# Attention and quantised feed-forward on one core: the order of TensorE's units regrouped by array shape

## The chip, the cores and the metric

The kernel runs on one core of a Trainium2 chip. The metric is the device time of one launch in microseconds, the median over runs. A profiled execution of the kernel before gives every row of the trace that is shown here.

## What is computed

Four sequences of 1024 rows of 128 numbers are normalised, go through attention with 16 heads of 64 columns, and through a quantised linear layer; the sum of input and both results is the output.

```
xn = layernorm(x)
q, k, v = heads(xn @ Wq), heads(xn @ Wk), heads(xn @ Wv)
w = softmax(q k^T / 64 + causal);  w = w * clip((key_no + span * 1024) / 33, 0, 1)
w = w / (sum(w) + 1e-8)
out = x + heads_back(w v) @ Wo + quantised(xn) @ (ternary - 1)^T + bias
```

## The kernel before, in words

**Rounds.** Two heads form a pair; there are 32 pairs, eight for each sequence (a "batch" in the code). The kernel runs about one round for each pair. Each engine has a written order of work (PE_PLAN, ACT_PLAN, DVE_PLAN, POOL_PLAN, SP_PLAN, lines 36 to 41, with _FIRST and _LAST for the ends), a list of words. `walk` goes through the list once for each pair i; a "+" behind a word means pair i + 1, a "-" pair i - 1. `happens` says in which pairs the rare words occur. Nothing but semaphores ties the engines together, and each engine works strictly in its order.

**TensorE's units.**

- Q, K (`projection`): the pair's queries and keys, 12 products of 512 columns together; V (`values`): 12 products of 256 columns; X0, X1 (`turn`): the transposed rows of the next sequence, three times in the run. All use the full array of 128 x 128.
- M0 to M11 (`max_unit`, L968): raw scores from which row maxima are taken, one product for each of the two heads. S0 to S11 (`scores_of`, L1006): the real scores by key block in transposed form, four products for each head, 512, 384, 256 or 128 columns wide (on the diagonal of the causal mask). Both use the array as two halves of 64 rows, one for each head.
- G3, G7, G11 (`value_products`, L1023): weights times values for tiles 0 to 3, 4 to 7 and 8 to 11 into the bank `pv`. D0, D1 (`denominators`, L1038): the sums of the weights for both halves of the queries. Both use the array as two halves of 64 columns.
- Y0, Y1 (`output_projection`, L1065; L1053 is the quantised product, which the last pair of a sequence puts ahead of it) and T (`turn_maxima`): the full array.

**Banks.** M, S, Q, K and V units go through `ring`, three slots of two banks. `slot_left` makes each unit wait until the unit three places earlier in the ring has been read: an S by ACT's exponential E, an M by DVE's maxima R, a Q or K by its low parts, a V by DVE's Vs.

```python
n = PLACE[name, i]
unit, j = IN_RING[n - NSLOT]
if unit[0] == "S":
    pe.wait_ge(exp_done, tiles_upto(j, int(unit[1:])))
elif unit[0] == "M":
    pe.wait_ge(max_read, j * NM + int(unit[1:]) + 1)
```

T, D, Y, X and W go through the one bank `beside` (`beside_left`): a Y waits until the D ahead has been turned into reciprocals, and a second Y until the first has been added to the output.

**The other engines.** ACT: E0 to E11 (exponentials, L567), copies of Q and K (L556), the logarithm and its exponential (ln, ex) of the denominators. DVE: R0 to R11 (L768 twice for a diagonal unit, L772 once for R4 to R7), low parts of Q and K (L744), Vs (L755), t, u, o (L792, L797, L804), the additions Ya0 and Ya1 to the output (L813), one step q of the quantisation in seven rounds of eight. GpSimd (POOL): L (causal selection, L474) and A (running sums of the weights, L495 to L501), the bias B. D0 waits for A3, D1 for A11; G3 to G11 wait for the selections L. SP issues the DMAs that place rows of maxima and keys.

Of the kernel before, what the change touches and what calls it, by code (L numbers as in the profile page):

```python
# [22 lines left out]
N_PAIRS = 32  # L23
# [82 lines left out]
IN_RING = [("X", -2)] + [u for u in PE_ORDER if u[0][0] in "QKSMV" or u == ("D1", LAST)]  # L106
IN_BESIDE = [u for u in PE_ORDER if u[0][0] in "THDYXWF" and u not in (("D1", LAST), ("Y1", LAST))]
# [23 lines left out]
def attention_ffn(nc, x_dram, wq_dram, wk_dram, wv_dram, wo_dram, span_dram, tern_dram, bias_dram,  # L131
# [11 lines left out]
    with ctx:  # L143
# [243 lines left out]
        def _(pool):  # L387
# [78 lines left out]
            pool.wait_ge(maxrow_done, 1)  # L466
            add_bias(0)
# [36 lines left out]
            for name, i in walk(POOL_PLAN, "", POOL_LAST):  # L504
                if name[0] == "L":
                    select(i, int(name[1:]))
                elif name[0] == "A":
                    add(i, int(name[1:]))
                else:
                    add_bias((6, 11, 14).index(i) + 1)  # L510

        @block.scalar
        def _(act):
# [29 lines left out]
            def turned_whole(b, c, src):  # L543

                if b > 0:
                    act.wait_ge(fq_step, (b - 1) * FQ_STEPS + 1)
                else:
                    act.wait_ge(x2_done, c + 1)
# [47 lines left out]
            for name, i in walk(ACT_PLAN, ACT_FIRST):  # L596
# [32 lines left out]
        def _(dve):  # L629
# [212 lines left out]
            for name, i in walk(DVE_PLAN, DVE_FIRST, DVE_LAST):  # L842
# [35 lines left out]
        def _(pe):  # L878
            t_ = nc.tensor

            def slot_left(name, i):
# [11 lines left out]
                elif unit == "V":  # L893
                    pe.wait_ge(v_done, j + 1)
                else:
                    pe.wait_ge(xf_done, 2)

            def beside_left(name, i):
# [13 lines left out]
                elif unit[0] == "X":  # L912
                    pe.wait_ge(x2_done, 2 * batch_of_turn(j) + int(unit[1:]) + 1)
# [164 lines left out]
            for name, i in PE_ORDER:  # L1078
# [27 lines left out]
                elif name[0] == "X":  # L1106
                    turn(batch_of_turn(i), int(name[1:]), beside[:, :])
# [28 lines left out]
```

## Time and profile before

| | |
|---|---|
| median of 3 runs | 1001.96 us (1001.88 to 1002.1) |
| the profiled execution | 1001.64 us, its span 999.9 us |
| granted clock, mean | 0.997 |
| PE busy | 985.0 us, 99%, 7121 instructions |
| DVE busy | 757.3 us, 76% |
| POOL busy | 707.5 us, 71% |
| ACT busy | 451.7 us, 45% |
| chain that ended last | PE 87%, DVE 8%, issue 2%, POOL 1%, ACT 1%, DMA 1% |

The profiled execution spends 1.74 us outside its span and lies 0.32 us under the median. In the timeline, a row's first number is the start from the span's beginning and the second its length. TensorE's products overlap in the pipeline and their ends are modelled, so the distance from one start to the next is what counts there. A row's "xN" merges N instructions of one line.

### The profile page before, as it was taken

To read this page: it belongs to the slowest core of one execution; us is meant where nothing else is said; L and a number is where in the kernel's file an instruction comes from. 1 tells how busy PE (TensorE), PEld (TensorE's weight loads), DVE (VectorE), ACT (ScalarE), POOL (GpSimd) and SP (SyncE) were. 2 spreads that over 40 slices of the span, in tenths; PEclk is the share of its full clock that TensorE was granted. 3 is DMA by queue.
4 is the path that set the end of the run, shared out by engine and by line. 5 is a ranking of instruction groups with operands and counts; after the bars stand their busy time and mean duration, and the time that the engine had idled before them with its cause. 6 is when DMAs were issued, how large, how long until landed. Compare 5 with 4: busy or idle time off the path is not lost.

```text
span 999.9 us, 19209 instructions
## 1 busy us (share of the span) xinstructions
PE 985.0 (99%) x7121; PEld 634.2 (63%) x7121; DVE 757.3 (76%) x1706; ACT 451.7 (45%) x607; POOL 707.5 (71%) x649
## 2 busy tenths in 40 slices
PE   8899999999999999999999999999999999999997
PEld 4666666666666666666666666666666666666654
DVE  7877888878788878777767777777877667777754
ACT  4344445444454444454443454444454444454442
POOL 8766867667767668767767767667767667777672
PEclk9999999999999999999999999999999999999999
DMA  6000000000000000000000000000000000000000
GB/s 176 3 2 2 2 1 3 2 3 2 2 22 3 2 2 2 1 3 2 3 12 13 1 3 2 2 2 3 1 2 23 3 2 2 1 2 2 2 2 22
DMA packets 16133, 8.52 MB, mean 9 GB/s; under 512 B 5404, under 2 KB 15644, under 8 KB 16040
## 3 DMA queue, kind: packets, MB, share of 16 engines
q1 hardware_dynamic: 15416, 7.15, 2.7%
q8 instruction: 57, 0.93, 0.4%
q14 instruction: 36, 0.29, 0.1%
q10 hardware_dynamic: 624, 0.14, 0.1%
HBM read 4.33 MB, written 2.10 MB: 6 GB/s over the span
## 4 chain that ended last, share of the span: by engine, by line
PE 87%; DVE 8%; issue 2%; POOL 1%; ACT 1%; DMA 1%; DVEq 0%; SPq 0%; ACTq 0%; POOLq 0%
PE pv L1023 25%; PE ring L1006 24%; PE ring L968 12%; PE beside L1065 7%; PE beside L1038 6%; PE ring L941 3%; PE ring L937 3%; PE ring L938 3%; DVE ring L768 3%; DVE v L755 2%; DVE beside L792 1%; PE ring L955 1%; PE beside L1053 1%; PE ring L956 1%; PE ring L957 1%
## 5 line engine op out<-in xcount | busy, mean ns | idle before, releaser
L567 ACT ACTIVATE prob<-ring 128x1024 f32<-128x1024 f32 (+3 forms) x384 | 293.6, 810 | 347.9 <-PE ring L1006 347.7
L501 POOL TENSOR_TENSOR psumd<-psumd,prob 128x512 f32<-128x512 f32 (+1 forms) x250 | 406.4, 1626 | 28.9 <-POOL psumd L501 1.3
L768 DVE CUSTOM_DVE_ANT_0 ring<-ring,causal 128x128 f32<-128x128 f32 (+3 forms) x512 | 240.3, 517 | 96.7 <-PE ring L968 96.2
L1006 PE MATMUL ring<-q,k 64*128 64x512 f32 (+3 forms) x2304 | 279.5, 347 | 1.7 <-DMA mrow<-maxrow 0.8
L1023 PE MATMUL pv<-prob,v 128*64 128x512 f32 (+3 forms) x1536 | 267.1, 490 | 0.0
L474 POOL TENSOR_SCALAR_AFFINE_SELECT prob<-prob 128x256 f32<-128x256 f32 x256 | 110.1, 432 | 216.1 <-ACT prob L567 214.1
L1006 PEld LDWEIGHTS ring<-q,k 64*128 64x128 f32 x2304 | 194.6, 185 | 37.3 <-DVE rowmax L768 5.1
L1023 PEld LDWEIGHTS pv<-prob,v 128*64 128x64 f32 x1536 | 104.9, 137 | 154.1 <-issue 142.4
L772 DVE TENSOR_REDUCE rowmax<-ring 128x2 f32<-128x1024 f32 x128 | 151.5, 1222 | 4.8 <-PE ring L968 1.3
L497 POOL TENSOR_TENSOR psumd<-prob 128x768 f32<-128x768 f32 (+1 forms) x63 | 132.6, 2105 | 24.3 <-ACT prob L567 19.1
L968 PE MATMUL ring<-k,q 64*128 64x512 f32 (+3 forms) x768 | 143.9, 410 | 4.2 <-DVE k L744 1.5
L1006 PE MATMUL ring<-mrow,kext 64*128 64x512 f32 (+3 forms) x768 | 133.6, 342 | 0.0
L968 PEld LDWEIGHTS ring<-k,q 64*128 64x128 f32 x768 | 64.9, 184 | 74.2 <-ACT prob L567 27.7
L556 ACT ACTIVATE q<-ring 128x1024 fp32r<-128x1024 f32 x32 | 32.9, 1028 | 143.6 <-PE ring L941 143.6
L1006 PEld LDWEIGHTS ring<-mrow,kext 64*128 64x128 f32 x768 | 73.2, 185 | 7.7
L1065 PE MATMUL beside<-wo,o 128*128 128x128 f32 x512 | 73.4, 286 | 1.1 <-DVE o L804 1.1
L768 DVE DVE_READ_ACCUMULATOR2_ANT rowmax<- 128x1 f32 x512 | 72.5, 142 | 0.0
L1065 PEld LDWEIGHTS beside<-wo,o 128*128 128x128 f32 x512 | 62.0, 191 | 13.9 <-issue 9.2
L792 DVE TENSOR_TENSOR beside<-beside,r 128x512 f32<-128x512 f32 x63 | 45.0, 715 | 32.9 <-ACT r L578 32.8
L744 DVE TENSOR_TENSOR q<-ring,q 128x1024 fp32r<-128x1024 f32 x32 | 39.1, 1222 | 40.1 <-ACT q L556 40.0
L1038 PE MATMUL beside<-psumd,ones 128*64 128x512 f32 x252 | 68.0, 617 | 0.9 <-POOL psumd L501 0.9
L937 PE MATMUL ring<-x,w 128*128 128x512 f32 x128 | 53.0, 414 | 0.0
(120 smaller groups left out, 947.0 us busy)
## 6 DMA issues: line engine op xcount, KB each, us to landing
kext<-kext SPq DMA_DIRECT2D x128, 4.0 KB, 1.7
out<-x_sb SPq DMA_DIRECT2D x8, 256.0 KB, 2.4
x_sb<-in_L_attn_query SPq DMA_DIRECT2D x3, 512.0 KB, 5.5
mrow<-maxrow SPq DMA_DIRECT2D x62, 4.0 KB
x_sb<-in_L_attn_query SPq DMA_DIRECT2D x2, 256.0 KB, 4.0
xn_sb<-in_L_attn_Wv SPq DMA_DIRECT2D x1, 512.0 KB, 5.5
wo<-in_L_attn_Wo SPq DMA_DIRECT2D x1, 512.0 KB, 7.0
xn_sb<-in_L_attn_Wq SPq DMA_DIRECT2D x1, 448.0 KB, 3.5
```

The source lines that it names most:

```text
L474: g.affine_select(out=d, in_=d, compare_op=ALU.is_ge, fill=0.0, base=0, pattern=[[0, 2], [1, P]], channel_multiplier=-1).then_inc(sel_done, 1)
L497: g.tensor_tensor(acc[:, :, lo:HALF], before[:, :, lo:HALF], pr[:, :, lo:HALF], ALU.add).then_inc(acc_done, 2)
L501: g.tensor_tensor(acc[:, :, lo:HALF], acc[:, :, lo:HALF], pr[:, :, lo:HALF], ALU.add).then_inc(acc_done, 1)
L567: a.activation(prob[n % NPROB][:, :, lo:HALF], ring[:, slot(f"S{t}", i), :, lo:HALF], ACT.Exp, scale=1.0 / DH).then_inc(exp_done, 1)
L768: last = v.tensor_tensor_reduce(out=ring[:, s, h, 0:n], in0=ring[:, s, h, 0:n], in1=causal[:, HALF - n:HALF], scale=1.0, scalar=MASKED, op ...
L772: last = v.tensor_reduce(dst[:, :, 0], ring[:, s, :, 0:n], axis=AX, op=ALU.max)
L937: t_.matmul(ring[:, s, c, :], w1[n][:, cols], xa[:, rows], start=True, stop=False)
L968: last = t_.matmul(ring[:, s, h, 0:n], q1[p][rows, j * P:(j + 1) * P], k1[p][rows, k0:k0 + n], start=True, stop=True)
L1006: last = t_.matmul(ring[:, s, h, lo:HALF], k[p][rows, keys], q[p][rows, cols], start=(at == 0), stop=(at == len(parts) - 1))
L1023: last = t_.matmul(pv[h * DH:(h + 1) * DH, lo:HALF], v_sb[i // 2 % 2][:, kb, i % 2 * 2 + h, :], prob[(i * NT + t) % NPROB][:, h, lo:HALF], ...
L1038: last = t_.matmul(out[h * DH:(h + 1) * DH, :], ones[:, :], psumd[c][:, h, :], start=True, stop=not direct)
L1065: last = t_.matmul(beside[:, k * P:(k + 1) * P], o_sb[c][:, k * P:(k + 1) * P], wo[:, i % NPB, :], start=not with_ffn, stop=(not with_ffn ...
```

## The change

The written orders are changed, and with them three details: the transposed rows X of the next sequence (both halves as one unit) go through the ring instead of `beside`; their unsplit copy xf is made by GpSimd as the sum of the two parts and not by two copies of ACT; and the first bias is added in round 0 instead of ahead of the rounds.

TensorE's steady round, with "|" at each change of the array's shape, before and after:

```
T Q K | G11 | M0 M1 S0 S1 S2 M2 | D1 | M3 S3 | V | S4 S5 M4 S6 M5 | Y1 | M6 M7 S7 | D0 G3 |
  M8 S8 S9 S10 M9 | Y0 | M10 M11 S11 | G7 |
T Q K | G11 D1 | M0 M1 S0 S1 S2 S3 S4 M2 M3 | Y0 V (X) Y1 | M4 S5 S6 M5 S7 M6 M7 | D0 G3 |
  M8 S8 S9 S10 M9 M10 M11 S11 | G7 |
```

```diff
-PE_PLAN = ("T Q+ K+ X0 X1 W G11- M0+ M1+ S0 S1 S2 M2+ D1- M3+ S3 V+ S4 S5 M4+ S6 M5+ Y1- M6+ M7+ S7 D0 G3 "
-           "M8+ S8 S9 S10 M9+ Y0 M10+ M11+ S11 G7")
-ACT_PLAN = "Z Qhi+ Khi+ X0 X1 E0 E1 E2 ln1- ex1- E3 E4 E5 E6 E7 ln0 ex0 E8 E9 E10 E11"
-DVE_PLAN = ("Tc Z Qlo+ Klo+ R0+ R1+ X0 X1 W R2+ R3+ t1- u1- Vs+ o1- R4+ R5+ Ya1- R6+ R7+ t0 u0 R8+ o0 q "
-            "R9+ R10+ Ya0 R11+")
-POOL_PLAN = "L0 A0 L1 A1 L2 A2 L3 A3 A4 A5 A6 A7 L8 L9 L10 L11 A8 A9 A10 A11 B"
+PE_PLAN = ("T Q+ K+ G11- D1- M0+ M1+ S0 S1 S2 S3 S4 M2+ M3+ Y0- V+ X Y1- M4+ S5 S6 M5+ W S7 M6+ M7+ D0 G3 "
+           "M8+ S8 S9 S10 M9+ M10+ M11+ S11 G7")
+ACT_PLAN = "Z Qhi+ Khi+ ln1- ex1- E0 E1 E2 E3 E4 X E5 E6 E7 ln0 ex0 E8 E9 E10 E11"
+DVE_PLAN = ("Tc Z Qlo+ Klo+ q R0+ R1+ t1- u1- o1- R2+ Ya0- R3+ Vs+ X R4+ Ya1- W R5+ R6+ R7+ t0 u0 R8+ o0 "
+            "R9+ R10+ R11+")
+POOL_PLAN = "L0 L1 L2 A0 L3 A1 A2 A3 B0 A4 A5 A6 A7 L8 A8 L9 L10 L11 A9 A10 A11 B xf"
 
 PE_FIRST = ("Q+ K+ I0+ I1+ M0+ M1+ M2+ I2+ M3+ I3+ M4+ I4+ M5+ I5+ H+ M6+ I6+ M7+ I7+ M8+ I8+ M9+ I9+ M10+ I10+ "
-            "M11+ S0+ S1+ T+ S2+ S3+ Q++ K++ V+")
+            "M11+ S0+ S1+ T+ S2+ S3+ Q++ K++ V+ S4+ M0++ I11+ M1++ I12+")
...
-ACT_FIRST = "xf0+ Qhi+ xf1+ Khi+ keys+ rest+ Hrow+ wv+ E0+ E1+ E2+ E3+ Qhi++ Khi++"
+ACT_FIRST = "xf0+ Qhi+ xf1+ Khi+ keys+ rest+ Hrow+ wv+ E0+ E1+ E2+ E3+ Qhi++ Khi++ E4+"
...
-PE_LAST = "T G11- S0 S1 S2 D1- S3 S4 S5 S6 Y1- S7 D0 G3 S8 S9 S10 S11 Y0 D1 F1 G7 G11 Y1"
+PE_LAST = "T G11- D1- S0 S1 S2 S3 S4 Y0- S5 Y1- S6 S7 D0 G3 S8 S9 S10 S11 Y0 D1 F1 G7 G11 Y1"
...
-DVE_LAST = "Tc t1- u1- o1- A5 Ya1- A6 A7 t0 u0 o0 A8 A9 Ya0 t1 u1 o1 Ya1"
+DVE_LAST = "Tc t1- u1- o1- q Ya0- A5 Ya1- A6 A7 t0 u0 o0 A8 A9 Ya0 t1 u1 o1 Ya1"
...
+BIAS_AT = (0, 6, 11, 14)
...
-    if name in ("X0", "X1"):
-        return i % PAIRS_OF_BATCH == 4 + int(name[1:]) and i < N_PAIRS - PAIRS_OF_BATCH
+    if name in ("X", "xf"):
+        return i % PAIRS_OF_BATCH == (4 if name == "X" else 5) and i < N_PAIRS - PAIRS_OF_BATCH
...
-IN_RING = [("X", -2)] + [u for u in PE_ORDER if u[0][0] in "QKSMV" or u == ("D1", LAST)]
-IN_BESIDE = [u for u in PE_ORDER if u[0][0] in "THDYXWF" and u not in (("D1", LAST), ("Y1", LAST))]
+IN_RING = [("X", -2)] + [u for u in PE_ORDER if u[0][0] in "QKSMVX" or u == ("D1", LAST)]
+IN_BESIDE = [u for u in PE_ORDER if u[0][0] in "THDYWF" and u not in (("D1", LAST), ("Y1", LAST))]
...
-            pool.wait_ge(maxrow_done, 1)
-            add_bias(0)
+            def rows_of_parts(b):
+
+                pool.wait_ge(x2_done, 2 * b + 2)
+                pool.wait_ge(fq_step, (b - 1) * FQ_STEPS + 1)
+                g.tensor_tensor(xf[:, :], x1[b % 2][:, :].bitcast(F32), x2[b % 2][:, :].bitcast(F32), ALU.add
+                                ).then_inc(xf_done, 2)
...
-                elif name[0] == "X":
-                    turned_high(batch_of_turn(i), int(name[1:]), beside[:, :])
-                    turned_whole(batch_of_turn(i), int(name[1:]), beside[:, :])
+                elif name == "X":
+                    for c in range(2):
+                        turned_high(batch_of_turn(i), c, ring[:, slot("X", i), c, :])
...
-                    quantise(i // NPB, i % NPB + 1)
-                elif name[0] == "X":
-                    turned(batch_of_turn(i), int(name[1:]), beside[:, :])
+                    quantise(i // NPB, i % NPB)
+                elif name == "X":
+                    for c in range(2):
+                        turned(batch_of_turn(i), c, ring[:, slot("X", i), c, :])
...
-                elif name[0] == "X":
-                    turn(batch_of_turn(i), int(name[1:]), beside[:, :])
+                elif name == "X":
+                    for c in range(2):
+                        turn(batch_of_turn(i), c, ring[:, slot("X", i), c, :])
```

## Rows read from the trace of the kernel before

**Rows 1.** Windows view: length, then busy time (instructions) per engine, PEclk, DMA.

```profile
903.98:933.72 29.74, 29.73 (x221) 19.25 (x219) 21.95 (x49) 13.59 (x18) 21.20 (x20) 1.00 0.01 2
...
36.00:39.00 3.00, 1.41 (x11) 0.86 (x9) 3.00 (x6) 0.13 (x1) 2.92 (x3) 0.96 0.01 1
39.00:42.00 3.00, 3.00 (x13) 2.30 (x14) 3.00 (x14) 0.00 (x0) 1.53 (x3) 0.50 0.01 3
```

**Rows 2.** Timeline of TensorE: start, length, line, operation, count.

```profile
914.11 0.39 PE L955 MATMUL ring<-wv,x 128*128 128x256 f32 x1
...
914.45 0.28 PE L957 MATMUL ring<-wv,x 128*128 128x256 f32 x1
...
915.51 0.28 PE L957 MATMUL ring<-wv,x 128*128 128x256 f32 x1
915.72 0.99 PE L1006 MATMUL ring<-q,k 64*128 64x512 f32 x6
...
916.76 0.89 PE L1006 MATMUL ring<-q,k 64*128 64x512 f32 x6
...
917.89 0.50 PE L968 MATMUL ring<-k,q 64*128 64x512 f32 x2
918.22 0.85 PE L1006 MATMUL ring<-q,k 64*128 64x512 f32 x6
...
919.13 0.40 PE L968 MATMUL ring<-k,q 64*128 64x512 f32 x2
919.46 1.16 PE L1065 MATMUL beside<-wo,o 128*128 128x128 f32 x8
920.55 0.74 PE L968 MATMUL ring<-k,q 64*128 64x512 f32 x4
```

**Rows 3.** Timeline of TensorE, M0 after G11, then M3 and S3 after D1.

```profile
909.37 0.50 PE L968 MATMUL ring<-k,q 64*128 64x128 f32 x4
...
913.28 0.50 PE L968 MATMUL ring<-k,q 64*128 64x512 f32 x2
913.62 0.45 PE L1006 MATMUL ring<-q,k 64*128 64x128 f32 x6
```

**Rows 4.** Timeline of TensorE, from S10 to Y0.

```profile
927.14 0.52 PE L1006 MATMUL ring<-q,k 64*128 64x256 f32 x6
...
927.73 0.38 PE L968 MATMUL ring<-k,q 64*128 64x256 f32 x2
928.04 1.16 PE L1065 MATMUL beside<-wo,o 128*128 128x128 f32 x8
```

**Rows 5.** Timeline of ScalarE: E6, then E8 to E10, then E9 alone.

```profile
919.34 1.02 ACT L567 ACTIVATE prob<-ring 128x1024 f32<-128x1024 f32 x1 [0.40 <-PE ring L1006]
...
926.65 2.22 ACT L567 ACTIVATE prob<-ring 128x1024 f32<-128x1024 f32 x3 [2.12 <-PE ring L1006]
...
927.58 0.80 ACT L567 ACTIVATE prob<-ring 128x768 f32<-128x768 f32 x1
```

**Rows 6.** Timeline of VectorE: R3, Vs, R4 with R5, Ya1, end of R9.

```profile
913.98 0.70 DVE L768 CUSTOM_DVE_ANT_0 ring<-ring,causal 128x512 f32<-128x512 f32 x1 [0.30 <-PE ring L968]
...
915.24 0.73 DVE L792 TENSOR_TENSOR beside<-beside,r 128x512 f32<-128x512 f32 x1
...
916.62 1.22 DVE L755 TENSOR_TENSOR v<-ring,vtab 128x1024 f32<-128x1024 f32 x1
...
918.54 2.37 DVE L772 TENSOR_REDUCE rowmax<-ring 128x2 f32<-128x1024 f32 x2
920.83 0.68 DVE L813 TENSOR_TENSOR x_sb<-x_sb,beside 128x512 f32<-128x512 f32 x1
...
929.04 0.14 DVE L768 DVE_READ_ACCUMULATOR2_ANT rowmax<- 128x1 f32 x1
```

**Rows 7.** Timeline of GpSimd: L0, and the last addition, A11.

```profile
911.93 0.41 POOL L474 TENSOR_SCALAR_AFFINE_SELECT prob<-prob 128x256 f32<-128x256 f32 x1 [3.92 <-ACT prob L567]
...
937.29 0.74 POOL L501 TENSOR_TENSOR psumd<-psumd,prob 128x256 f32<-128x256 f32 x1 [0.43 <-POOL psumd L501]
```

More of the change, by code:

```diff
@@ L79, in happens @@
     if name == "q":
-        return i % PAIRS_OF_BATCH < PAIRS_OF_BATCH - 1
+        return i % PAIRS_OF_BATCH > 0
     if name == "Z":
@@ L83, in happens @@
     if name == "B":
-        return i in (6, 11, 14)
+        return i in BIAS_AT[1:]
+    if name == "B0":
+        return i == BIAS_AT[0]
     if name == "store":
@@ L508, in _ @@
                     add(i, int(name[1:]))
+                elif name == "xf":
+                    rows_of_parts(batch_of_turn(i - 1))
                 else:
-                    add_bias((6, 11, 14).index(i) + 1)
+                    add_bias(BIAS_AT.index(i))
         @block.scalar
@@ L541, in turned_high, with turned_whole @@
                 a.activation(x1[b % 2][:, c * HALF:(c + 1) * HALF], src, ACT.Copy).then_inc(x1_done, 1)
[L543 to L548, printed above, removed]
+            def turned_whole(c, src):
+                act.wait_ge(x2_done, c + 1)
                 a.activation(xf[:, c * HALF:(c + 1) * HALF], src, ACT.Copy).then_inc(xf_done, 1)
@@ L604, in _ @@
                     inverses(i, int(name[2:]))
-                elif name[0] == "X":
-                    turned_high(batch_of_turn(i), int(name[1:]), beside[:, :])
-                    turned_whole(batch_of_turn(i), int(name[1:]), beside[:, :])
+                elif name == "X":
+                    for c in range(2):
+                        turned_high(batch_of_turn(i), c, ring[:, slot("X", i), c, :])
                 elif name[:2] == "xf":
-                    turned_whole(0, int(name[2:]), ring[:, slot("X", -2), int(name[2:]), :])
+                    turned_whole(int(name[2:]), ring[:, slot("X", -2), int(name[2:]), :])
                 elif name == "rest":
@@ L672, in turned @@
                 cols = slice(c * HALF, (c + 1) * HALF)
-                dve.wait_ge(x1_done if b == 0 else xf_done, 2 * b + c + 1)
+                dve.wait_ge(x1_done, 2 * b + c + 1)
                 v.tensor_tensor(x2[b % 2][:, cols], src, x1[b % 2][:, cols].bitcast(F32), ALU.subtract
@@ L894, in slot_left @@
                     pe.wait_ge(v_done, j + 1)
+                elif j < 0:
+                    pe.wait_ge(xf_done, 2)
                 else:
-                    pe.wait_ge(xf_done, 2)
+                    pe.wait_ge(x2_done, 2 * batch_of_turn(j) + 2)
             def beside_left(name, i):
@@ L911, in beside_left @@
                     pe.wait_ge(y_added, halves_upto(j, int(unit[1:])))
-                elif unit[0] == "X":
-                    pe.wait_ge(x2_done, 2 * batch_of_turn(j) + int(unit[1:]) + 1)
                 else:
```

## The prediction, made before the changed kernel ran

> **What bounds the kernel now.** The windows view comes first. In a steady round of 29.74 us TensorE is busy for 29.73, DVE for 21.95, GpSimd for 21.20, ACT for 13.59 [rows 1], so a round is what TensorE's order takes. A busy TensorE is not one at its peak, however: what it loses stands between the starts of its instructions, and for that I read its timeline unit by unit. There are two kinds of loss.
>
> *A change of the array's shape.* V's pieces follow each other every 0.118 us: nine steps from 914.45 to 915.51. Twelve would take 1.41, but V takes 1.61 until S4 starts: some 0.10 is lost as it starts and 0.09 as it leaves. S4, first after the change, takes 1.04 (915.72 to 916.76), while S6, as wide and inside its shape, takes 0.91 or 0.92 (918.22 to 919.13): 0.12 lost in the restart. M5, a pair as wide as those of S6 (0.23 each), takes 0.33 before Y1: 0.10 on the way in [rows 2]. So one excursion from the row shape into the full array and back costs 0.10 + 0.20 + 0.12 = 0.42 us. D1's excursion: 0.10 in and 0.09 out (taken as for M5 and V), and M3 after it 0.34 for a pair of 0.23 [rows 3], 0.11: together 0.30.
>
> *A slot that is still being read.* M9 may only start when E8 has read S8's slot. E8 ends at 926.65 + 1.03 = 927.68 [rows 5], M9's first instruction is at 927.73, and Y0 follows 0.31 later [rows 4], for a pair of 256 columns that takes 0.12, with 0.09 for the change behind it. The other 0.10 is M9's own start: its weights were not loaded ahead. So **a unit that was held streams 0.15 us after its release**, and I call that its effective start. M4, behind V's slot and so behind Vs, shows the same from the other side: S5 takes 1.13 for 0.92, and M4 0.33 for 0.23 [rows 2], a wait of 0.31 in all.
>
> **The change, part by part, in a steady round.**
>
> *1. Fewer changes of shape.* The full-array units inside the scores (V, Y1, Y0) were three excursions and become one: 2 x 0.42 = 0.84 saved. D1 joins G11: 0.30 saved. Sum -1.14 us. The products themselves are the same, moved. The Trainium skill, "TensorEngine Tiling (Array Packing)", Key Properties, says that changing the tiling mode drains TensorE; these rows agree with it, and by that rule alone a round would take 28.60.
>
> *2. The excursions were also pauses for the readers of the ring.* The same page, PSUM Bottleneck, says that tiling speeds up TensorE but not the evacuation of PSUM. What the rows make of that is worked out here from the readers' own times; by the page's rule alone no number follows. I lay the measured durations into the new order, with three slots.
>
> (a) After G3: M8 S8 S9 S10 M9 M10 M11 S11. M9's effective start is 927.83, as before. M10 takes S9's slot, so it waits for E9, which ends at 927.58 + 0.80 = 928.38 [rows 5]: effective 928.53 in place of 927.83 + 0.12 = 927.95, **wait 0.58**. M11 waits for E10: three exponentials end at 926.65 + 2.22 = 928.87 [rows 5], effective 929.02 in place of 928.53 + 0.17 = 928.70, **0.32**. S11 waits for R9, ended at 929.04 + 0.14 = 929.18 [rows 6]: 929.33 in place of 929.02 + 0.23, **0.08**. Today Y0 stands behind M9 and covers all of these.
>
> (b) S0 S1 S2 S3 S4 in a row. An exponential starts 1.12 after its S (E6 919.34, S6 918.22 [rows 2, 5]), the first lasts 1.03, the second ends 0.70 later (928.38 less 927.68). Counted from S0, S3 starts effectively at 1.12 + 1.03 + 0.15 = 2.30, held by E0, where M2 stands today with the same wait: no difference. S4 is held by E1: 2.15 + 0.70 + 0.15 = 3.00. S3 takes 0.49 less the 0.09 of the change behind it (913.62 to 914.11 [rows 2, 3]), so S4 would have started at 2.70: **0.30**.
>
> (c) S5 S6 M5 S7. S7 now takes S5's slot: E5 ends 1.12 + 1.02 after S5, effective 2.29, against 0.92 + 0.92 + 0.23 = 2.07: **0.22**.
>
> (d) M6 M7. M7 now takes M5's slot, and R5 stands at the end of an unbroken run of DVE. Ya0 starts about 1.1 after Y0's effective start (seven pieces, and some 0.3 for the result, an estimate). On DVE the next instruction starts 0.09 before the last has ended (R4 and R5 take 2.37 together for 1.23 each), so from start to start Ya takes 0.68 - 0.09 = 0.59, R3 1.26 (913.98 to 915.24), Vs 1.22 - 0.09 = 1.13, R4 1.14 [rows 6]. R5 could then start at 1.1 + 0.59 + 1.26 + 1.13 + 1.14 + 0.59 = 5.81. TensorE: Y0 0.90 (1.09 less its two losses), V 1.41, Y1 0.90, change 0.19, M4 0.23, S5 0.92, S6 0.92: M5 at 5.47; R5 starts 0.55 after it (R4 918.54, M4's effective start 917.99 [rows 2, 6]), at 6.02, ends at 7.25, M7 effective at 7.40. Without R5, M7 would follow S7 (3.63 + 2.29 = 5.92), 0.92 and M6's 0.23: 7.07. **Wait 0.33.**
>
> Sum of new waits: 0.58 + 0.32 + 0.08 + 0.30 + 0.22 + 0.33 = +1.83 us. M4's old wait goes, because its slot is now M2's, read long before: -0.31.
>
> *3. What stays hidden.* D1 right behind G11 needs A11 earlier. A11 ends at 938.03 [rows 7]; its round's T, where the windows are cut, stood at 933.72 and D1 would start where M0 stands now, 5.39 behind T (909.37 less 903.98 [rows 1, 3]), at 939.11. Slack 1.1 us, minus 0.15; and A8 is pulled ahead of L9 to L11. The bias additions and xf, at most 3.0 us each (four times A11's 0.74 for 256 columns of two operands), come in six rounds and go into GpSimd's idle time before L0, 3.92 us [rows 7]; B0 alone stands in mid-round, once. If that cover were gone, D1 would be late by the difference. q on DVE now stands ahead of R0, in the time of G11 and D1. ACT loses six copies. ln and ex now stand ahead of E0 and fit between D1's end and E0, which must wait for S0 in any case: 0. SP's DMAs of the row maxima get a microsecond more. All this at 0, between -0.1 and +0.2 a round.
>
> *4. The ends.* Y0 of round 0 moves out of the first round and that of round 30 into the last: 0. The fill-in products I11 and I12 and the earlier S4, M0, M1 may keep the clock up in the start: today TensorE is busy for 1.41 of 3 us and then runs at a granted clock of 0.50, the lower level of 1.2 GHz, for the next 3.00 us [rows 1], which costs up to 1.5. I take -1. The three rounds with X have ACT's and DVE's reading of X inside the run of (d); I take +0.3 each, +1. Together 0, bounds -3 and +3.
>
> **The sum.** +1.83 - 0.31 - 1.14 = +0.38 us in each of 31 rounds: +11.8. 1001.64 (the profiled execution, 0.32 under the median) + 11.8 = 1013.4, **1013.5 us**. Each wait rests on three or four starts read to 0.05; 0.25 on their sum is 8 us. Its own range is 1004 to 1022.
>
> **The rivals.**
>
> *The drain alone counts.* None of the new waits shows, since a reader catches up inside the run: -1.45 x 31 = -45, **957 us**. For it: ACT is busy 13.59 of 29.74 us, DVE 21.95 [rows 1]. Against it: M9 and M4 show a held unit waiting to the hundredth although both engines have idle time. It decides wherever the new waits come to less than 1.45 a round, against the 1.83 found. If only group (a) failed to show, 0.98 less, the time would be 1013.5 - 30 = **983 us**. Chance 0.14 for all of this side.
>
> *An even trade.* Waits of 1.45: 1002 us. 0.06.
>
> *GpSimd becomes the bound.* D1 is held by A11. It needs GpSimd 1 us later than now against T; L1 and L2 ahead of A0 wait for later exponentials, and the bunch at S5 starts late. Were it 1 us beyond the slack, 31 us more on the forecast: **1044 us**. 0.05.
>
> *The forecast*, slower by the waits of the bunches: 0.75.
>
> The three runs lie within 0.22 us; a difference of 0.2%, 2 us, is about what a measurement of this kernel can tell from no change. Faster 0.15, same 0.06, slower 0.79. Range 998 to 1022: it leaves out the rivals at 957, 983 and 1044 and holds the even trade.
>
> **What would show it.** Right: a steady round of 30.1 us; M10 held by E9 and M11 by E10 in the waits, some 0.9 us a round together; M7 by R5; S4 by E1; M4's wait for Vs gone; D1 not waiting for POOL. Wrong: rounds near 28.6 (no waits), or a wait of D1 for psumd, or M7's wait over 1 us, which would mean that DVE bounds the stretch from Ya0 on.

## The result, and the profile after

| | before | changed |
|---|---|---|
| median | 1001.92 us (1000.88 to 1002.1, 4 runs) | 1012.76 us (1012.75 to 1012.78, 4 runs) |
| ratio, 95% interval | 1 | 1.0106 (1.0086 to 1.0125) |
| span of the profiled execution | 999.9 us | 1011.0 us |

The change costs 10.8 us. The spans of the profiled executions differ by 11.1 us. The first part of the page of the changed kernel shows TensorE's busy time all but unchanged (985.0 before) and its share down from 99% to 97%:

```profile
PE 984.5 (97%) x7125; PEld 627.0 (62%) x7125; DVE 753.7 (75%) x1706; ACT 450.0 (45%) x601; POOL 707.3 (70%) x652
```

The windows view of one steady round (from one T to the next, as in [rows 1]) and of the stretch in the start where the clock had been low:

```profile
36.00:39.00 3.00, 2.82 (x19) 1.74 (x19) 2.87 (x7) 1.13 (x2) 2.36 (x4) 1.00 0.02 4
39.00:42.00 3.00, 3.00 (x20) 2.12 (x20) 2.75 (x12) 0.00 (x0) 2.06 (x1) 1.00 0.00 0
...
883.15:913.33 30.18, 29.75 (x221) 18.99 (x220) 22.09 (x49) 13.62 (x18) 21.05 (x20) 1.00 0.01 2
```

This round's T stands at 883.15 and the next T at 913.31 (the window is 0.02 longer), so a steady round takes 30.16 us in place of 29.74; the six rounds ahead of the last, which hold neither X nor a quantised product, take 30.15 to 30.20. VectorE is busy for 22.09 us of the round (21.95 before), the other engines no longer than before. In the start the granted clock stays at 1.00 (2.4 GHz) and TensorE is busy for 2.82 of the 3 us from 36 and for all of the next 3, where it had been busy for 1.41 and then run at 0.50 [rows 1].

The timeline of TensorE in that round answers to [rows 2 to 4]. First D1 and M0, then the stretch from S3 to S5:

```profile
888.42 1.03 PE L1047 MATMUL beside<-psumd,ones 128*64 128x512 f32 x4
889.38 0.49 PE L977 MATMUL ring<-k,q 64*128 64x128 f32 x4
...
891.93 0.55 PE L1015 MATMUL ring<-q,k 64*128 64x128 f32 x6
...
892.63 0.96 PE L1015 MATMUL ring<-q,k 64*128 64x512 f32 x6
...
894.16 1.16 PE L1074 MATMUL beside<-wo,o 128*128 128x128 f32 x8
895.08 0.36 PE L964 MATMUL ring<-wv,x 128*128 128x256 f32 x1
...
896.59 1.05 PE L1074 MATMUL beside<-wo,o 128*128 128x128 f32 x8
897.57 0.50 PE L977 MATMUL ring<-k,q 64*128 64x512 f32 x2
897.91 0.87 PE L1015 MATMUL ring<-q,k 64*128 64x512 f32 x6
```

Y0 to V takes 0.92 and V to Y1 1.51, where V alone in the scores took 1.61 [rows 2]. Y1, entered from the full array, takes 0.98 until M4, against 1.09. The whole stretch from Y0 to M4 is 3.41, against 1.09 + 1.61 + 1.09 = 3.79 for the three units in their old places: 0.38 less, which is two times the 0.19 of one excursion's two edges. So the changes of shape gave back what was worked out. But S3 takes 0.70 until S4, against 0.49 until V in [rows 2, 3]: S4 waits for E1.

Now the second half of the round, with M5, S7, M6 and M7, D0, and then M9 to S11:

```profile
899.76 0.41 PE L977 MATMUL ring<-k,q 64*128 64x512 f32 x2
900.14 0.96 PE L1015 MATMUL ring<-q,k 64*128 64x512 f32 x6
...
901.18 0.93 PE L977 MATMUL ring<-k,q 64*128 64x512 f32 x4
902.04 1.08 PE L1047 MATMUL beside<-psumd,ones 128*64 128x512 f32 x4
...
907.63 0.38 PE L977 MATMUL ring<-k,q 64*128 64x256 f32 x2
908.33 0.99 PE L977 MATMUL ring<-k,q 64*128 64x384 f32 x4 [0.32 <-ACT prob L575]
909.15 0.53 PE L1015 MATMUL ring<-q,k 64*128 64x128 f32 x6
```

M5 to S7 is 0.38 for a pair of 0.23; M6 and M7 together take 0.86 until D0, for 0.46 of products and 0.09 of change. M9 to M10 is 0.70, where a 256-column pair is 0.12. The row of 908.33 merges M10 and M11, which take 0.82 until S11, for 0.17 + 0.23.

The timeline of ACT in the same place, E8 to E10:

```profile
906.55 2.22 ACT L575 ACTIVATE prob<-ring 128x1024 f32<-128x1024 f32 x3 [2.12 <-PE ring L1015]
```

E10 ends at 906.55 + 2.22 = 908.77 and E9 0.49 earlier, at 908.28 (the distance of the two in [rows 5]: 928.87 less 928.38). M10's first instruction is at 908.33, 0.05 behind. The timeline of DVE, Ya1 and R5:

```profile
899.49 0.68 DVE L821 TENSOR_TENSOR x_sb<-x_sb,beside 128x512 f32<-128x512 f32 x1
900.33 1.23 DVE L780 TENSOR_REDUCE rowmax<-ring 128x2 f32<-128x1024 f32 x1 [0.16 <-PE ring L977]
```

R5 ends at 900.33 + 1.23 = 901.56, and M7, in the row of 901.18, has its first instruction at 901.61.

The waits view names the same engines. It lists TensorE's weight loads (PEld ring L977 is M, L1015 is S) and its products (PE); the columns are the sum in us, the count and the longest:

```profile
PEld ring L977 <- ACT prob L575: 31.8, 102, 0.5
...
PEld ring L977 <- DVE rowmax L780: 15.0, 38, 0.6
PEld ring L1015 <- ACT prob L575: 14.1, 56, 0.4
...
PE ring L977 <- ACT prob L575: 9.7, 31, 0.3
```

The same view of the kernel before, where M stands on L968:

```profile
PEld ring L968 <- ACT prob L567: 27.7, 48, 0.8
...
PEld ring L968 <- DVE v L755: 14.9, 31, 0.9
```

Two cautions go with such rows. The view counts the idle time of the engine named, so its sums lie under those from the starts; and PEld can be idle while TensorE multiplies. The 27.7 us of before are mostly of that kind. 31 of the 48 are M3's weight load, idle for 0.81 us in each round while D1 ran, and E1, which it is put down to, had ended before (even E2 was done at 913.04):

```profile
913.28 0.19 PEld L968 LDWEIGHTS ring<-k,q 64*128 64x128 f32 x2 [0.81 <-ACT prob L567]
```

That is some 25 us which cost nothing; what is left of the 27.7 is about 2.6 us, among it M9 behind E8. After, M's and S's weight loads wait 31.8 and 14.1 us for exponentials, M's 15.0 for maxima (R5), and in 31 places M's products stand idle as well, 9.7 us (M10 behind E9). No wait for Vs is left among the large ones. So the difference between the two kernels is larger than the view's sums say.

Where the new round's 0.42 us come from, by starts, each as effective start less the unheld one:

| held unit, by | predicted | measured |
|---|---|---|
| M10, E9 | 0.58 | 0.58 |
| M11, E10 | 0.32 | 0.32 |
| S11, R9 | 0.08 | 0.11 |
| S4, E1 | 0.30 | 0.30 |
| S7, E5 | 0.22 | 0.25 |
| M7, R5 | 0.33 | 0.31 |
| sum | 1.83 | 1.87 |
| M4's old wait gone | -0.31 | -0.31 |
| fewer changes of shape | -1.14 | -1.14 |
| a round | +0.38 | +0.42 |

The measured column is read as in the prediction: S4 892.63 + 0.10 less (891.93 + 0.10 + 0.40); S7 900.14 + 0.10 less (899.76 + 0.23); M7 from the 0.86 of M6 and M7 less 0.46 and 0.09; M10 908.33 + 0.10 less (907.63 + 0.10 + 0.12). M11 and S11 are from the single starts 908.82 and 909.15 of the trace. The row of the fewer changes of shape is taken as the remainder. Read by itself it comes to -1.16: 0.38 in the stretch from Y0 to M4; 0.16 at G11 and D1 (3.16 together, 886.22 to 889.38, against 2.31 and 1.01 before); and the three edges ahead of D1, Y1 and Y0 (0.10, 0.10, 0.09) and three restarts of M3, M6 and M10 (0.11 each) that no longer occur.

Outside the steady rounds the two kernels differ with both signs; by the starts of T the terms are these. 31 rounds of +0.42 are +13.0. The first three rounds together are 1.9 shorter than before (T of round 0 to T of round 3: 88.65 against 90.56 us) and so 3.2 below what +0.42 each would give; of these up to 1.5 are the clock, 0.9 Y0, which comes back behind the last T (37.35 us to the end of the span against 36.45), and some 0.8 stay unexplained. The three rounds with X take 1.3, 1.9 and 1.2 more than a steady one, against 0.45 in each of two rounds before: +1.5 in all. The rest, some -1.2, is rounds 3 and 7 to 11: before, they took up to 0.3 us each more than their like further on (round 10 took 29.99 in place of 29.73), and now they do not. The sum is 11.0 of the 11.1 us.

### The profile page after: what moved, and what is told of

It reads as the page before. It is cut to its first block, busy times and chain, and to the rows that moved or that the text cites. A ratio compares the mean times of both kernels' runs of the same rounds, so it can differ in the third digit from the quotient of the medians.

```text
span 1011.0 us, 19214 instructions
## 1 busy us (share of the span) xinstructions
PE 984.5 (97%) x7125; PEld 627.0 (62%) x7125; DVE 753.7 (75%) x1706; ACT 450.0 (45%) x601; POOL 707.3 (70%) x652
## 4 chain that ended last, share of the span: by engine, by line
PE 84%; issue 5%; DVE 4%; ACT 4%; POOL 2%; DMA 0%; ACTq 0%; DVEq 0%; POOLq 0%
PE pv L1032 25%; PE ring L1015 25%; PE ring L977 9%; PE beside L1074 6%; PE beside L1047 6%; ACT prob L575 3%; PE ring L950 3%; PE ring L946 3%; PE ring L947 3%; PE ring L965 1%; PE ring L964 1%; PE ring L966 1%; POOL psumd L510 1%; DVE ring L776 1%; DVE rowmax L780 1%
## 5 line engine op out<-in xcount | busy, mean ns | idle before, releaser
L776 DVE CUSTOM_DVE_ANT_0 ring<-ring,causal 128x128 f32<-128x128 f32 (+3 forms) x512 | 237.2, 519 | 82.0 <-PE ring L977 81.6
L1015 PE MATMUL ring<-q,k 64*128 64x512 f32 (+3 forms) x2304 | 288.3, 355 | 2.0 <-DVE k L752 0.5
L483 POOL TENSOR_SCALAR_AFFINE_SELECT prob<-prob 128x256 f32<-128x256 f32 x256 | 105.2, 423 | 200.8 <-ACT prob L575 198.4
L1015 PEld LDWEIGHTS ring<-q,k 64*128 64x128 f32 x2304 | 187.1, 185 | 49.3 <-ACT prob L575 14.1
L977 PE MATMUL ring<-k,q 64*128 64x512 f32 (+3 forms) x768 | 146.2, 403 | 14.5 <-ACT prob L575 9.7
L1015 PE MATMUL ring<-mrow,kext 64*128 64x512 f32 (+3 forms) x768 | 133.4, 342 | 0.0
L977 PEld LDWEIGHTS ring<-k,q 64*128 64x128 f32 x768 | 69.2, 183 | 93.7 <-issue 32.6
L581 ACT ACTIVATE lnden<-beside 128x512 f32<-128x512 f32 x63 | 37.7, 599 | 97.0 <-PE beside L1047 97.0
L1015 PEld LDWEIGHTS ring<-mrow,kext 64*128 64x128 f32 x768 | 73.0, 185 | 8.2
L1074 PE MATMUL beside<-wo,o 128*128 128x128 f32 x512 | 70.7, 281 | 0.9 <-DVE o L812 0.9
L788 DVE TENSOR_REDUCE maxrow<-beside 16x128 fp32r<-16x256 f32 x32 | 13.2, 412 | 72.7 <-PE beside L985 72.7
```

The source lines that it names most:

```text
L483: g.affine_select(out=d, in_=d, compare_op=ALU.is_ge, fill=0.0, base=0, pattern=[[0, 2], [1, P]], channel_multiplier=-1).then_inc(sel_done, 1)
L776: last = v.tensor_tensor_reduce(out=ring[:, s, h, 0:n], in0=ring[:, s, h, 0:n], in1=causal[:, HALF - n:HALF], scale=1.0, scalar=MASKED, op ...
L977: last = t_.matmul(ring[:, s, h, 0:n], q1[p][rows, j * P:(j + 1) * P], k1[p][rows, k0:k0 + n], start=True, stop=True)
L1015: last = t_.matmul(ring[:, s, h, lo:HALF], k[p][rows, keys], q[p][rows, cols], start=(at == 0), stop=(at == len(parts) - 1))
L1074: last = t_.matmul(beside[:, k * P:(k + 1) * P], o_sb[c][:, k * P:(k + 1) * P], wo[:, i % NPB, :], start=not with_ffn, stop=(not with_ffn ...
```

## The experiments

Two theories stood against each other. **Waits:** a round is work, plus changes of shape, plus the time in which a unit waits for a slot still being read; gathering the full-array work took away pauses in which the readers caught up. **Drain alone:** only the changes of shape count, and the new kernel is slower for some other reason (GpSimd's order, D1 early, xf). Times of the kernel before in these comparisons are 1001.9 to 1002.2 us.

### One part of the change alone: D1 behind G11

```diff
-"T Q+ K+ X0 X1 W G11- M0+ M1+ S0 S1 S2 M2+ D1- M3+ S3 V+ ..."
+"T Q+ K+ X0 X1 W G11- D1- M0+ M1+ S0 S1 S2 M2+ M3+ S3 V+ ..."
```

(in the kernel before; DVE takes X0, X1 and W ahead of R0, and PE_LAST is changed likewise)

> The kernel before with one part of the change alone: D1 stands behind G11, so two changes of shape fewer in a round; the order of the ring's units is the same. Theory (waits take the place of the pauses): D1's excursion also covered M3, which needs S1's slot, and S3, which needs S2's. The changes of shape give back 0.30 to 0.34 us a round, M3 now waits about 0.5 us for E1 and S3 about 0.26 for E2: a steady round of 30.2 us instead of 29.74, 12 to 15 us slower, 1014 to 1017 us. Rival (only the changes of shape count): 0.30 to 0.34 us less in each of 31 rounds, about 991 us. Rival (GpSimd is the bound for an early D1): D1 waits for psumd by more than 0.3 us a round, and M3 does not wait.

Measured: 1019.25 us (1017.42 to 1019.8), ratio 1.0166 (1.0150 to 1.0181), 2 us above the range expected. Two changes of shape fewer, and 17 us slower. The timeline of TensorE, M2, M3, S3 and V:

```profile
898.11 0.44 PE L968 MATMUL ring<-k,q 64*128 64x384 f32 x2
898.80 0.51 PE L968 MATMUL ring<-k,q 64*128 64x512 f32 x2 [0.26 <-ACT prob L567]
899.29 0.55 PE L1006 MATMUL ring<-q,k 64*128 64x128 f32 x6
...
899.94 0.39 PE L955 MATMUL ring<-wv,x 128*128 128x256 f32 x1
```

M2 to M3 takes 0.69 and M3 to S3 0.49 (0.17 and 0.23 of products): M3 waits 0.52 for E1 and S3 0.26 for E2, as laid out. A steady round is 30.19 us, 0.45 over that of before: 14 us. The rest is outside the steady rounds. X0 and X1 now hold up D1 in `beside` (X rounds 0.9 to 1.2 over the steady one, against 0.45, some 3 us in all). D1 did not wait for psumd in the steady rounds; it did once, in the last pair, for 1.4 us. The clock of the start was low for longer than before. Against these stand shorter rounds at the start and from 9 to 11, as in the changed kernel. The drain alone would have given 991.

### One part undone: Y0 back between M9 and M10

```diff
-"... M2+ M3+ Y0- V+ X Y1- ... S8 S9 S10 M9+ M10+ M11+ S11 G7"
+"... M2+ M3+ V+ X Y1- ... S8 S9 S10 M9+ Y0 M10+ M11+ S11 G7"
```

(Ya0 on DVE goes back between R10 and R11; PE_LAST and DVE_LAST likewise)

> The changed kernel with Y0 back between M9 and M10 of its own round, the rest as changed: ten changes of shape in a round. Theory of the waits, laid out over the whole round: the waits of M10, M11 and S11 (0.98 us) go, the excursion costs 0.4 us, but V now follows M3 directly and takes S4's slot while E4 still reads it, about 0.76 us of wait: a steady round of 30.3 to 30.4 us against 30.16, 1017 to 1022 us. Rival (the waits behind M9 are the whole of the loss, as the group-by-group sum would have it): 0.56 us a round less than the changed kernel, about 995 us. Rival (only changes of shape count): 0.4 us a round more, which is near the first; V's wait and M10's tell them apart: by this rival M10 waits as before and V not at all.

Measured: 1021.03 us (1020.58 to 1021.65), ratio 1.0187 (1.0172 to 1.0202). A steady round is 30.33 to 30.38 us (the six ahead of the last). The timeline of TensorE, M2 and M3, V's first piece, then M9, Y0, and M10 with M11:

```profile
897.54 0.56 PE L977 MATMUL ring<-k,q 64*128 64x384 f32 x4
898.82 0.39 PE L964 MATMUL ring<-wv,x 128*128 128x256 f32 x1 [0.71 <-ACT prob L575]
...
911.39 0.38 PE L977 MATMUL ring<-k,q 64*128 64x256 f32 x2
911.70 1.16 PE L1074 MATMUL beside<-wo,o 128*128 128x128 f32 x8
912.79 0.68 PE L977 MATMUL ring<-k,q 64*128 64x384 f32 x4
```

V starts 1.28 after M2, for 0.17 + 0.23 + 0.09: it waits 0.79 for E4. M9 to Y0 is back at 0.31; M10 and M11 take 0.51 until S11 (913.30), for 0.40 of products and 0.11 of restart, and wait for nothing. So this shows both that the wait of M10, M11 and S11 was the missing pause of Y0, and that undoing one group only moves the wait: a sum made group by group (1.01 us of waits gone for an excursion of 0.42, in 31 rounds: -18) would have promised 995. The steady rounds make 6 of the 8.3 us over the changed kernel; some 3 are a wait for GpSimd's sums in the last pair, 4.5 us here and 1.5 there.

### Both kernels with readers half as long

```diff
-a.activation(prob[n % NPROB][:, :, lo:HALF], ring[:, slot(f"S{t}", i), :, lo:HALF], ACT.Exp,
+a.activation(prob[n % NPROB][:, 0:1, lo:HALF], ring[:, slot(f"S{t}", i), 0:1, lo:HALF], ACT.Exp,
...
-                    for h in range(2):
+                    for h in range(1):
                         last = v.tensor_tensor_reduce(
...
-                    last = v.tensor_reduce(dst[:, :, 0], ring[:, s, :, 0:n], axis=AX, op=ALU.max)
+                    last = v.tensor_reduce(dst[:, 0:1, 0], ring[:, s, 0:1, 0:n], axis=AX, op=ALU.max)
```

(the untouched halves of `prob` and of the maxima are set once, to 1 and 0; TensorE's work is the same)

> The kernel before with its readers of the ring made about half as long: every exponential and every row maximum works on one head of the two (the other head's weights stay at 1 and its maxima at 0; the products are all made). Theory: its order has few waits to lose (M9 for E8, M4 for Vs, M2 for E0), so a round falls from 29.74 to about 29.2 us: about 983 us. Its 14 changes of shape stay. Rival (TensorE's order is not what the readers hold up): no change, 1002 us.

> The changed kernel with the same halved readers. Theory: its waits (M10, M11, S11, S4, S7, M7) go and only the fewer changes of shape stay, so the verdict turns round: a steady round of 28.6 to 28.7 us against about 29.2 for the kernel before with the same readers, 14 to 20 us faster than that one, about 967 us. Rival (the new order is slower for another reason: its POOL order, xf, the order of DVE): it stays 10 us or so slower than the kernel before with halved readers.

Measured: 978.18 us for the order of before (ratio 0.9768, 0.9743 to 0.9793) and **966.53 us** for the new order (0.9646, 0.9630 to 0.9662). Steady rounds: 28.96 and 28.55 us. The verdict turns round: with the same halved readers the new order is 11.7 us faster, the intervals apart (14 to 20 had been expected). So the new order is not slower in itself; it is slower with readers of this length. That the gain is 0.41 us a round and not 1.14 is again the waits: they are all but gone with the order of before, and not all gone with the new one. The waits of the order of before, M for Vs:

```profile
PEld ring L971 <- DVE v L755: 1.5, 4, 0.9
```

(Its M behind exponentials still counts 24.9 us, 31 times, the longest 0.8: this is M3's weight load beside D1 alone, which costs nothing.)

And of the new order, M and S behind exponentials and maxima:

```profile
PEld ring L980 <- ACT prob L575: 11.8, 62, 0.2
...
PEld ring L1018 <- DVE rowmax L776: 6.6, 31, 0.5
...
PEld ring L980 <- DVE rowmax L780: 5.6, 30, 0.2
```

M's wait for Vs has fallen from 14.9 us to 1.5 with the order of before; with the new one 62 M units still wait for an exponential and 61 units for a maximum. In starts, M9 to S11 and S11 to G7 are some 0.6 us a round over their products there, and M6 with M7 0.07, against the 0.73 between 1.14 and 0.41. I had put the order of before at 983: its rounds were to be 29.2, and its waits were worth more than I had thought.

### GpSimd's order as before

```diff
-POOL_PLAN = "L0 L1 L2 A0 L3 A1 A2 A3 B0 A4 A5 A6 A7 L8 A8 L9 L10 L11 A9 A10 A11 B xf"
+POOL_PLAN = "L0 A0 L1 A1 L2 A2 L3 A3 B0 A4 A5 A6 A7 L8 L9 L10 L11 A8 A9 A10 A11 B xf"
```

> The changed kernel with GpSimd's order as before (each addition behind its selection, A8 behind L11). Theory: GpSimd is not the bound and D1 has about 2 us of slack in the new order, 1 us or more in the old one: no change, 1012 to 1014 us, D1 waits for nothing. Rival (GpSimd bounds D1 when it stands right behind G11): D1 waits for psumd, 1015 us or more.

Measured: 1014.95 us (1014.90 to 1014.99), 2.2 over the changed kernel's 1012.76 and 1 over the range expected. The steady round is 30.16 as with the new order. Rounds 2, 7 and 15 take 0.3 to 0.5 more and round 12 takes 0.7 less. The largest single piece is D1 of the last pair, in the timeline of TensorE:

```profile
978.28 1.08 PE L1047 MATMUL beside<-psumd,ones 128*64 128x512 f32 x4 [1.41 <-POOL psumd L510]
```

It waits 1.41 us for A11, which it does not in the changed kernel. So GpSimd is not what makes the steady round longer, but its slack is not large, and the order given to it was worth 2 us. Which of its moves did it (L1 and L2 ahead of A0, or A8 ahead of the later selections) no run tells.

### The cost of a change of shape by itself

In the changed kernel, in the midst of full-array work ahead of K, where nothing waits, a tiny product is added whose result K overwrites.

```diff
+                if name == "K":
+                    t_.matmul(ring[0:64, s, 0, 0:2], w1[n][:, cols.start:cols.start + 64], x1[i // NPB % 2][:, 0:2],
+                              start=True, stop=True)
```

> The changed kernel with one product of two columns added ahead of K in every pair, on 64 columns of the array, in the middle of full-array work: two changes of shape more a round, nothing waits there. The added value is overwritten by K. With 0.09 to 0.10 us for each change and 0.05 and 0.10 for the two starts without weights loaded ahead, 0.34 us more a round than the same product on the full array: 10 to 12 us above that run. Rival (a change of shape costs little, the waits are all): within 3 us of it.

> The same added product on all 128 columns: no change of shape. One more weight load and product, 0.05 to 0.11 us a round: 2 to 4 us above the changed kernel, 1014 to 1017 us.

Measured: 1016.49 and 1016.43 us: the same, 3.7 us or 0.115 us a round over the changed kernel. The timeline of TensorE shows why, Q's last product, the added one, and K's first two; with 64 columns:

```profile
887.84 0.39 PE L953 MATMUL ring<-x,w 128*128 128x512 f32 x1
888.07 0.17 PE L940 MATMUL ring<-x,w 128*64 128x2 f32 x1
888.10 0.47 PE L949 MATMUL ring<-x,w 128*128 128x512 f32 x1
888.41 0.39 PE L950 MATMUL ring<-x,w 128*128 128x512 f32 x1
```

and with 128 the same four stand at 887.98, 888.21, 888.23 and 888.55. The product follows Q's last after 0.23 in both: no gap of 0.09. **A single product on 64 columns left no sign of a change of shape.** The 0.115 us are 0.03 until K's first and 0.08 behind it, where K's second comes after 0.31 and not 0.23. My test had missed its object. The next one uses both halves of columns, as D and G do:

```diff
+                if name == "K":
+                    for h in range(2):
+                        t_.matmul(ring[h * DH:(h + 1) * DH, s, 0, 0:2], ones[:, :], ident[:, 0:2], start=True, stop=True)
```

> The run with one extra product on 64 columns showed no gap around it and the same time as on 128 columns, so it did not change the array's shape. Here the extra work ahead of K is a pair of fp32 products of two columns, one on each half of 64 columns, as D1 makes them; K overwrites what they write. If using the second half is what changes the shape, the pair costs two changes a round more than the same pair on the full array: 0.3 us a round, 8 to 12 us over the control run. Rival (what D and G cost at their edges comes from their place next to row-shaped or waiting work, not from the shape): within 3 us of the control.

> Control: the same pair of fp32 products on the full array of 128 columns, twice. No change of shape; four weight loads more a round, 0.1 us each: 1022 to 1028 us if nothing absorbs them, 1016 at least.

Measured: 1026.05 and 1026.68 us. By the expectation's letter the rival had won. But the timeline (again Q's last, the added products, K's first and second) shows the gap:

```profile
896.52 0.40 PE L953 MATMUL ring<-x,w 128*128 128x512 f32 x1
896.85 0.28 PE L941 MATMUL ring<-ident,ones 128*64 128x2 f32 x4
897.06 0.50 PE L949 MATMUL ring<-x,w 128*128 128x512 f32 x1
897.40 0.39 PE L950 MATMUL ring<-x,w 128*128 128x512 f32 x1
```

0.33 from Q's last product to the pair, which is 0.23 without a change, in the control too (its added products are fp32 as well: 897.32 to 897.55). So it is not the type that makes the gap. The pair's four instructions take 0.21 until K's first, and K's second comes 0.34 after that. These two cannot be laid to the change as they stand: in the runs without one, K's second comes after 0.31 to 0.32. The control was none for the work, since the two halves run side by side (0.11 us for the pair's four instructions), which its four on the full array cannot (0.11 each). The last run makes the pair twice (`for h in (0, 1, 0, 1)`):

> The run with a pair of products on the two halves ahead of K took 0.415 us a round more than the changed kernel (13.3 us over 32 rounds); its control was no control, since products on the full array cannot run side by side. Here the pair is made twice, with no further change of shape. If changes of shape cost what the edges of D1, V and Y showed, the second pair costs only its work, two passes of 0.08 to 0.11 us: 5 to 7 us over the run with one pair (1031 to 1033), and the first pair's other 0.2 us a round are its two changes. Rival (a change costs nothing, the work is all): the second pair costs as much as the first, 13 us, about 1039.

Measured: 1029.52 us (1029.38 to 1029.58), 3.5 us over the run with one pair (5 to 7 had been expected, 13 by the rival): 0.11 us a round for a pair's work. The first pair cost 13.3 / 32 = 0.415, so its two changes of shape cost **0.31 us**. This takes it that without a change the first pair would cost what the second does; on the full array one added product cost 0.115 and four cost 0.435, 0.11 each, so there the first costs no more than the others. The prediction took 0.30 for D1's excursion, which is from the row shape and back and not from the full array; the two prices are alike, not the same thing.

### The start without fill-in products

```diff
-            "M11+ S0+ S1+ T+ S2+ S3+ Q++ K++ V+ S4+ M0++ I11+ M1++ I12+")
+            "M11+ S0+ S1+ T+ S2+ S3+ Q++ K++ V+ S4+ M0++ M1++")
```

> The changed kernel without the two fill-in products I11 and I12 in the start. If it is these that keep TensorE's clock up there, the granted clock falls to 0.5 for some 3 us near 39 us as in the kernel before, and the time is 1 to 1.5 us longer (1014). If it is the earlier S4 that does it, nothing changes (1012 to 1013).

Four executions: 1012.21, 1012.35, 1019.63 and 1019.70 us. The profiled one was a long one, and the windows view shows TensorE at the lower level of its clock in two stretches of the start:

```profile
20.00:37.00 17.00, 17.00 (x50) 8.60 (x49) 10.90 (x29) 4.55 (x5) 10.28 (x7) 0.51 0.19 46
...
47.00:51.00 4.00, 4.00 (x21) 3.34 (x22) 4.00 (x10) 0.00 (x0) 0.57 (x1) 0.57 0.00 0
```

The first stretch, 17 us, begins ahead of anything that was changed; the second, in the place where the kernel before has it, is what was looked for. But two executions took 1012.2 and 1012.4, under the changed kernel's own time, so the fill-in products are not shown to bring anything. Nor can the two long ones be laid to their absence: executions some 7 us longer than their fellows, at a mean granted clock of 0.99, also came up in kernels that have them (998.82 against 992.2, 1023.07 against 1016.5, 1032.56 against 1026.0) and in the kernel before (1008.7 against 1002.0). Inconclusive; what the first term of "the ends" is worth stays open.

### An order that beats both

From the theory: keep the full-array stretch and D1 beside G11, and place the units so that no slot is wanted while a slow reader has it.

```diff
-"... Y1- M4+ S5 S6 M5+ W S7 M6+ M7+ D0 G3 M8+ S8 S9 S10 M9+ M10+ M11+ S11 G7"
+"... Y1- M4+ S5 S6 S7 M5+ D0 M6+ M7+ S8 G3 M8+ S9 M9+ S10 S11 M10+ M11+ G7"
-DVE  "... q R0+ R1+ t1- u1- o1- ... R7+ t0 u0 R8+ o0 R9+ R10+ R11+"
+DVE  "... R0+ R1+ t1- u1- q o1- ... R7+ t0 u0 R8+ R9+ o0 R10+ R11+"
-POOL "L0 L1 L2 A0 L3 A1 A2 A3 B0 A4 A5 A6 A7 L8 A8 L9 L10 L11 A9 A10 A11 B xf"
+POOL "L0 A0 B0 L1 A1 L2 L3 A2 A3 B A4 xf A5 A6 A7 L8 L9 A8 L10 A9 L11 A10 A11"
```

(W moves behind G11, on DVE behind Klo)

> The changed kernel's code with other orders: full-array stretch and D1 beside G11 as changed, but the units of the ring are placed so that a slow reader's slot is not wanted at once (S7 ahead of M5, D0 and G3 set as covers between M5, S8 and M8, and so on; ten changes of shape in a round). Theory (a round is work plus changes plus waits for slots): the waits fall from some 1.8 to 0.9 us a round for two more changes; laid out over the round it gives 29.5 us, against 29.74 before and 30.16 after: about 992 us, range 988 to 998, faster than both. Rival (only fewer changes of shape are of use): ten changes must lie above eight, over 1012 us. Rival (the waits move to other units): 1000 to 1010 us.

Measured: **992.29 us** (the median of six executions, 992.19 to 998.82), ratio 0.9924 (0.9904 to 0.9943), 9.6 us faster than the kernel before and 20.5 faster than the changed one. Ten changes of shape in a round, and a steady round of 29.42 to 29.48 us (the six ahead of the last), 0.71 under the changed kernel's. Two more changes of shape cost 0.3 to 0.4 by the prices above, so the waits fell by about 1.0 to 1.1 of their 1.87, an estimate. The timeline of TensorE, S7, M5, D0, M6 with M7, S8:

```profile
910.48 0.89 PE L1015 MATMUL ring<-q,k 64*128 64x512 f32 x6
...
911.38 0.44 PE L977 MATMUL ring<-k,q 64*128 64x512 f32 x2
911.75 1.08 PE L1047 MATMUL beside<-psumd,ones 128*64 128x512 f32 x4
912.76 0.73 PE L977 MATMUL ring<-k,q 64*128 64x512 f32 x4
913.33 0.89 PE L1015 MATMUL ring<-q,k 64*128 64x512 f32 x6
```

S7 to M5 0.90, M5 to D0 0.37, of which 0.09 is the change: neither is held for long. M6 and M7 take 0.57 for 0.46 and a restart of 0.11: M5's slot is now taken by S8, and D0 (1.01 with its changes) stands in between. R5 is done only just in time (0.05 us before S8's weights are loaded), and S8 loses next to nothing by it. GpSimd's and VectorE's orders were changed along, so the 20 us are those of the whole set.

## Why the prediction was right

**The verdict and its size.** 1013.5 us was forecast, 1012.76 measured; it lies in the forecast's own range, and the steady round (30.16 against 30.12) and each held unit came out as worked out, so it is the mechanism that was right and not the number alone. The faster rivals (957, 983) are ruled out by the timeline, the one with GpSimd (1044) by the steady rounds, in which D1 never waited for psumd. The one such wait of the execution, 1.5 us, is that of D0 in the last pair, and the kernel before has it too, with 0.85.

**Step 1, fewer changes of shape, -1.14.** Right, by the rows of after (-1.16); the runs with extra products give a like price, 0.31 us for two changes. The Trainium skill, "TensorEngine Tiling (Array Packing)", Key Properties, says that a change of tiling mode drains TensorE; this trace agrees, with 0.09 to 0.10 at the edge and as much in the start behind it.

**Step 2, the pauses, +1.83.** Right unit by unit (the table above), sum 1.87; no unit was off by more than 0.03. The same page of the Trainium skill, PSUM Bottleneck, says that tiling speeds up TensorE but not the evacuation of PSUM. This case agrees: the readers of a slot took as long as before (1.02 us for the exponential of a full unit, 1.22 to 1.23 for its maxima), and with readers half as long the order that loses wins by 11.7 us. One detail of (d) was worded wrongly: R5 was called the end of an unbroken run of DVE, but DVE idled for 0.16 us ahead of it (the row of 900.33 comes 0.16 after Ya1's end), as its own sum 5.81 against 6.02 said. What holds M7 is that M5, whose slot it takes, stands only three places ahead of it in the ring, not the run.

**Step 2, the old wait of M4, -0.31.** Right: M4 to S5 is 0.34 with the restart of a change, no wait for Vs.

**Step 3, what stays hidden, 0.** Right for the steady rounds. The room for D1 was larger than worked out: GpSimd's idle time before L0 grew from 3.92 to 6.41 us.

```profile
891.95 0.41 POOL L483 TENSOR_SCALAR_AFFINE_SELECT prob<-prob 128x256 f32<-128x256 f32 x1 [6.41 <-ACT prob L575]
```

A11 had ended at 885.54 and D1 started at 888.42, 2.9 us later, where the prediction had 1.1.

**Step 4, the ends, 0 with bounds of 3.** Right in sum only by the breadth of the bounds: 31 rounds made +13.0 and the spans differ by 11.1, so the ends gave -1.9. Of the terms, X's +1 came out as +1.5. The clock's -1 was near in the profiled executions (it stayed up), but no run shows what decides it. The prediction did not have the long rounds 3 and 7 to 11 of the kernel before (-1.2) nor the last 0.8 of what the first three rounds gave back; why either came about stays open.

**The sum** came out 0.7 us high: +0.04 a round too little (1.2 us), 1.9 us at the ends too much. That these two nearly cancel is luck, though each by itself is small beside the 10.8.

## What to carry to other kernels

A unit that seems to interrupt the array's work may be the pause in which the readers of PSUM catch up; before gathering such units, lay each one's slot, its reader's end and 0.15 us of restart into the new order, over the whole round, since a wait taken away in one place comes back at the next slot. Count a change of shape by itself (here 0.15 to 0.19 us each: 0.31 for two, 1.14 for six) and weigh it against the wait that it covers. And where an order loses by waits, keep its gain and re-space it: that, with the orders of GpSimd and VectorE fitted to it, was worth 20 us here.

## What the runs showed of the hardware that was not expected

- A product on 64 of 128 columns in the lower half of the outputs alone cost what one on 128 columns cost (1016.49 and 1016.43 us) and left no gap; the gap of 0.10 us came only when both halves were used. The single product was fp32r and the pair fp32. The type by itself makes no gap on the full array (0.23 us to the control's fp32 products); a single fp32 product on 64 columns was not tried. So the edge at G and D belongs to the use of the two halves, as far as these forms show it.
- Two such products side by side started 6 to 7 ns apart; a pair of them cost 0.11 us, a product of two columns on the full array 0.115 us. The single starts of the trace fit a price set by the loading of the weights: loads of 128 columns follow each other every 0.11 us there, those of 64 columns every 0.055 us, two for each product of the pair. No run varied it: in the two runs with a single product, its own load stood beside Q's last product, so its width could not show.
- A unit held by a semaphore started 0.05 us after the release and streamed 0.15 us after it, whichever engine released it: so for E8, E9, E1 and R5. For S11 behind R9 the weights were loaded 0.05 us and the first product started 0.08 us after the release.
- A row of the waits view on PEld is not yet a wait of TensorE: M3's weight load stood idle for 0.81 us in every round of the kernel before while D1 was being multiplied.
